# Moving instructions between rounds in an eight-stage transformer kernel on one core

## The chip, the core and the metric

The kernel runs on one core of a Trainium2 chip. The core has five engines that run their own instruction lists in order and meet through semaphores: PE (matmuls, with a separate list of weight loads, PEld), DVE (vector work), ACT (activation functions and copies), POOL (further vector work) and SP (here only transfers). Transfers are issued from the queues of SP and ACT, for weights also of POOL. PE writes its results to PSUM, from where DVE and ACT read them. The metric is the device time of one execution in microseconds (us).

## The reference

The input x is 8 batches of 256 tokens with 256 channels, float32. Four attention blocks alternate with four feed-forward blocks, each with a norm ahead and a residual behind:

```python
x = x + _L0_attn_a_ref(_layernorm(x), Wq, Wk, Wv, Wo)              # 16 heads of 16, softmax
x = x + _L0_ffn_ref(_layernorm(x), weight, scale_weight, bias)     # one linear layer
x = x + _L0_attn_b_ref(_layernorm(x), Wq, bq, Wk, bk, ...)         # 4 heads of 64, softmax
x = x + _L0_ffn_ref(...)
x = x + _L1_attn_a_ref(...)    # retention: scores * decay mask, no softmax, two rms norms behind
x = x + _L1_ffn_ref(...)       # silu(x W1) * (x W3), Hadamard transform, W2, 1024 hidden
x = x + _L1_attn_b_ref(...)    # per token: attention among 32 half-heads, softmax, difference
x = x + _L1_ffn_ref(...)
```

In the last attention each token has its own 32 x 32 score matrix (`einsum('bnqd,bnkd->bnqk', q, k)`): softmax over it, and the second half of the heads is subtracted, times a factor, from the first.

## The kernel before

The stages are named A0S (first attention), F1, B0 (second attention), F3, R1 (retention), F5, B1 (token attention) and F7. Every stage handles the 8 batches one after the other as a software pipeline written out by hand. Time is counted in slots (rounds); a batch takes 8 slots (ROUNDS). For each slot, `together` calls the `at_slot(g)` of every stage in turn on every engine, where g is the slot relative to the start of the stage. Inside, a line such as

```python
for b in due(g, -5):
    v_out(b)
```

emits step `v_out` of batch b when g = 8 b - 5. So the number says in which slot a step stands in the engine's list, and the order of the lines says in which order the steps of a slot stand. Nothing else sets an order: every engine works through its list and waits at each step for the semaphores named in `wait(name, batch, count)`. `wait("xres", b - 3, 1)` for example waits until batch b - 3 has its residual. A waiting step holds up everything behind it on its engine, transfers of that queue too. "High" and "low" are the two parts into which a float32 operand is split for PE: ACT writes the high part, DVE subtracts it to get the low part, and a product takes three matmuls.

Second attention (B0), batch b. PE: x is transposed (`x_turned`, slot -13), keys (-11), queries (-9), values (`v_out`, -5), scores (0, 2), turned row maxima (`max_turned`, 4; it waits for the values copy of batch b + 1, since both use the accumulator pb), shifted scores (6, 8), weights times values (`attend`, 9, 11), output product (14). DVE: `maximum`, `max_low`, the copy of the values with bias (`v_out`, -4), the division by the sums (`heads_out`, 10 and 12; the second product of `attend` waits for the first division), `a_low`, `residual`. F3 uses the same slots for its own batches, and POOL prepares the weights of later stages here (`prepare`, `butterfly`, `cut_mask`).

Retention (R1). One score round per slot: PE `scores_t`, DVE `masked`, PE `attend`. Between them stand the projections of later batches (`x_turned` -16, `q_out` -13, `k_out` -11, `v_out` -9) and the outputs of earlier ones. `to_tokens` and `k_out` share the accumulator pa: `k_out(b)` waits for "normed" of batch b - 3, which DVE's `heads_out` of the second half (slot 13) raises. Queries and keys go through DRAM: SP stores them (`store`, -12 and -10) and fetches them in two halves (`load_q`, `load_k`).

Token attention (B1), batch b, two score halves h. PE: `scores` (slot h), transposed probabilities (`turned`, 8), products with the values (`attend`, 9), transposed output (18), output product `y_out` (24), x transposed (-16), queries, keys, values (-14 to -12). DVE: `less_maximum` clamps the scores from PSUM (L1572), takes the maximum (L1574) and subtracts it (L1576); `weights_of` sums the exponentials (L1580), inverts, scales and multiplies (L1589). ACT: `probs` is the exponential, `turned` the copy of the channels (b_DT), `heads_out` the two copies of the heads (b_O), followed by their store, `load_k` six of the 16 key transfers per batch (SP issues ten), and the copies of q, k and v; `y_out` of an older batch waits for the copy of v (b_V), as both use pb. SP: `load_out` fetches the heads back, `load_v` the values, and the stores of q, k, v. POOL: `rstd_of`, `clipped` (waits for the load of the heads), `row_bias`, `token_heads` (with a power step, L778).

Of the kernel before, what the change touches and what calls it, by code (L numbers as in the profile page):

```python
# [36 lines left out]
TT = S // P  # L37
# [116 lines left out]
def build(nc, T, out):  # L154
    ctx = ExitStack()
    with ctx:
# [314 lines left out]
        def _(sp):  # L471
# [25 lines left out]
            for s, st in enumerate(STAGES):  # L497
                if st.kind in ("ffn0", "wide"):
                    at[s] = lambda g: None
                if st.kind == "narrow":  # L500

                    def narrow(s, st):
# [50 lines left out]
                        def at_slot(g):  # L553
                            if st.name == "attn_a0":
                                for b in due(g, 9):
                                    max_rows(b)
                                for b in due(g, -13):
                                    store(b, "kl", "kstore", "kload", KT, k_dram)
                                for b in due(g, -11):
                                    store(b, "ql", "qstore", "qload", QT, q_dram)  # L560
                                for half in range(2):
                                    for b in due(g, 4 * half - 8):
                                        load_q(b, half)
                                    for b in due(g, 4 * half - 6):
                                        load_k(b, half)
                            else:
                                for b in due(g, -12):
                                    store(b, "ql", "qstore", "qload", QT, q_dram)
                                for b in due(g, -10):
                                    store(b, "kl", "kstore", "kload", KT, k_dram)  # L570
                                for half in range(2):
                                    for b in due(g, 4 * half - 8):
                                        load_q(b, half)
                                    for b in due(g, 4 * half - 7):
                                        load_k(b, half)
# [3 lines left out]
                if st.kind == "tokens":  # L579
                    def tokens(s):  # L580
# [40 lines left out]

                        def at_slot(g):
                            for b in due(g, -7):
                                load_k(b)
                            for b in due(g, 9):
                                load_out(b)
                            for b in due(g, -7):
                                load_q(b)
                            for b in due(g, 2):
# [252 lines left out]
        def _(act):  # L882
# [13 lines left out]
            def narrow(s, st):  # L896
# [69 lines left out]
                def at_slot(g):  # L966
                    if ret:
                        for b in due(g, -8):
                            v_out(b)
# [14 lines left out]
                        for b in due(g, 26):  # L984
                            a_high(b)
                        for b in due(g, -15):
                            x_high(b)
                        for b in due(g, -13):
                            q_high(b)
                        for b in due(g, -11):  # L990
                            k_high(b)
# [85 lines left out]
            def tokens(s, st):  # L1077
# [52 lines left out]

                def at_slot(g):
                    for b in due(g, 8):
                        turned(b)
                    for h in range(TT):
                        for b in due(g, 9):
                            heads_out(b, h)
                    for b in due(g, 1):
                        probs(b, 0)
                    for b in due(g, 9):
                        store_out(b)  # L1140
                    for b in due(g, -16):
                        high(b, x_pair(s, b), pa, "xT", "vp", 1, "xh")
                    for b in due(g, 18):
                        high(b, aT, OT[1], "aT", "y", 1, "ah")
                    for b in due(g, -14):
                        out(b, "qp", "qstore", b1_qt, pb, "qev")
                    for b in due(g, -6):
                        load_k(b)
                    for b in due(g, -13):
                        out(b, "kp", "kstore", b1_kt, pa, "kev")  # L1150
                    for b in due(g, 3):
                        probs(b, 1)
                    for b in due(g, -12):
# [84 lines left out]
        def _(dve):  # L1238
# [12 lines left out]
            def narrow(s, st):  # L1251
# [127 lines left out]
                def at_slot(g):  # L1379
                    if ret:  # L1380
                        for b in due(g, 26):
                            a_low(b)
                        for b, r in running(g, 0):
                            masked(b, r)
                        for b in due(g, -15):
                            x_low(b)
                        for b in due(g, -12):
                            low(b, QT, pb, "qh", "ql")
                        for b in due(g, -10):
                            low(b, KT, pa, "kh", "kl")  # L1390
# [39 lines left out]
            def wide(s, st):  # L1430
# [70 lines left out]
                def at_slot(g):  # L1501
                    for t in range(TT):
                        for b in due(g, 1 + 2 * t):
                            maximum(b, t)
                    for b in due(g, 5):
                        max_low(b)
                    for b in due(g, -12):
                        x_low(b)
                    for c in range(CT):
                        for b in due(g, 10 + 2 * c):  # L1510
                            heads_out(b, c)
                    for b in due(g, 13):
                        a_low(b)
# [4 lines left out]
                    for b in due(g, -8):  # L1518
                        low(b, b0_Q, pb, "qh", bq, "ql")
                    for b in due(g, -4):  # L1520
                        v_out(b)
                    for b in due(g, -21):
# [15 lines left out]
            def tokens(s, st):  # L1538
# [62 lines left out]

                def at_slot(g):
                    for b in due(g, 24):
                        residual(b)
                    for b in due(g, -16):
                        low(b, x_pair(s, b), pa, "xh", "xl")
                    for b in due(g, 1):
                        less_maximum(b, 0)
                    for b in due(g, 2):
                        weights_of(b, 0)  # L1610
                        less_maximum(b, 1)
                    for b in due(g, 18):
                        low(b, aT, OT[1], "ah", "al")
                    for b in due(g, 13):
                        square_sums(b)
                    for b in due(g, 4):
                        weights_of(b, 1)
                    for b in due(g, -20):
# [168 lines left out]
        def _(pe):  # L1787

            def narrow(s, st, turn, channels_out, tokens_out, w):
# [155 lines left out]
                def at_slot(g):  # L1945
                    if ret:
# [15 lines left out]
                        for b in due(g, -13):  # L1962
                            q_out(b)
                        for b in due(g, -11):
                            k_out(b)
# [30 lines left out]
            def wide(s, turn, channels_out, tokens_out, w):  # L1996
# [102 lines left out]
                def at_slot(g):  # L2099
# [6 lines left out]
                    for c in range(CT):  # L2106
                        for b in due(g, 9 + 2 * c):
                            attend(b, c)
                    for b in due(g, -13):
                        x_turned(b)  # L2110
# [8 lines left out]
                    for b in due(g, -5):  # L2119
                        v_out(b)  # L2120
                return at_slot

            def tokens(s, st, turn, channels_out, tokens_out, w):
# [79 lines left out]

                def at_slot(g):
                    for b in due(g, 24):
                        y_out(b)
# [5 lines left out]
                    for h in range(TT):  # L2212
                        for b in due(g, 9):
                            attend(b, h)
                    for h in range(TT):
                        for b in due(g, h):
                            scores(b, h)
                    for b in due(g, 18):
# [233 lines left out]
```

## Time and profile before

| what | value |
|---|---|
| median of 3 runs | 1123.61 us (1122.81 to 1127.87) |
| the profiled execution | 1126.71 us, span 1124.9 us |
| PE busy | 915.9 us (81%) |
| PE weight loads | 776.4 us (69%) |
| DVE busy | 695.5 us (62%) |
| ACT busy | 367.3 us (33%) |
| POOL busy | 317.2 us (28%) |
| mean granted clock of PE | 0.896 |

The span reaches from the first to the last instruction of the profiled execution. Busy shares are means over stages: the second attention lies at about 250 to 464 us, retention at 464 to 603, F5 at 603 to 769, the token attention at 769 to 963 and F7 behind it, with overlaps at the seams. The granted clock is given as a share of full speed; 1.00 is 2.4 GHz and 0.50 is 1.2 GHz.

### The profile page before, as it was taken

To read this page: it belongs to the slowest core of one execution; us is meant where nothing else is said; L and a number is where in the kernel's file an instruction comes from. 1 tells how busy PE (TensorE), PEld (TensorE's weight loads), DVE (VectorE), ACT (ScalarE), POOL (GpSimd) and SP (SyncE) were. 2 spreads that over 40 slices of the span, in tenths; PEclk is the share of its full clock that TensorE was granted. 3 is DMA by queue.
4 is the path that set the end of the run, shared out by engine and by line. 5 is a ranking of instruction groups with operands and counts; after the bars stand their busy time and mean duration, and the time that the engine had idled before them with its cause. 6 is when DMAs were issued, how large, how long until landed. Compare 5 with 4: busy or idle time off the path is not lost.

```text
span 1124.9 us, 21059 instructions
## 1 busy us (share of the span) xinstructions
PE 915.9 (81%) x8018; PEld 776.4 (69%) x8018; DVE 695.5 (62%) x1291; ACT 367.3 (33%) x663; POOL 317.2 (28%) x352
## 2 busy tenths in 40 slices
PE   3589988787777678778877999997678874799998
PEld 2466665566666566656656999995566653799997
DVE  4468777646665567887775554536766767454443
ACT  2136554444222222233434332233222321332332
POOL 4202222224568474211111112100154443330000
PEclk9779998898898989898888999999777887899999
DMA  8745541001100002455440000022454445100000
GB/s 227 232 139 157 147 119 55 12 11 38 48 20 1 1 1 66 131 152 163 120 123 1 2 1 1 1 57 51 82 113 85 86 90 82 33 15 20 10 20 20
DMA packets 148580, 76.78 MB, mean 68 GB/s; under 512 B 108992, under 2 KB 139712, under 8 KB 148480
## 3 DMA queue, kind: packets, MB, share of 16 engines
q1 hardware_dynamic: 139376, 65.47, 23.1%
q0 software_dynamic: 1424, 4.98, 1.5%
q10 hardware_dynamic: 7680, 4.98, 1.5%
q8 instruction: 64, 1.05, 0.4%
q14 instruction: 36, 0.29, 0.1%
HBM read 45.77 MB, written 29.36 MB: 67 GB/s over the span
## 4 chain that ended last, share of the span: by engine, by line
PE 58%; DVE 26%; issue 7%; ACT 4%; SPq 2%; DMA 1%; POOL 1%; ACTq 0%; DVEq 0%; POOLq 0%
PE SC L380 17%; PE pb L380 8%; PE OT L380 8%; PE pa L380 4%; DVE mx L1315 3%; PE OT L2173 3%; PE OT L1890 3%; DVE OS L1488 2%; PE SC L1843 2%; PE SC L1872 2%; PE OT L2088 2%; PE SC L2161 2%; DVE pr L1576 2%; PE pa L2356 2%; DVE m L1574 2%
## 5 line engine op out<-in xcount | busy, mean ns | idle before, releaser
L380 PE MATMUL SC<-xT_h,w_h 128*128 128x256 f32 x512 | 148.3, 290 | 13.8 <-DVE xT_l L1737 11.5
L380 PE MATMUL SC<-xT_l,w_h 128*128 128x256 f32 x512 | 146.4, 286 | 0.0
L380 PE MATMUL SC<-xT_h,w_l 128*128 128x256 f32 x512 | 145.7, 285 | 0.0
L380 PEld LDWEIGHTS SC<-xT_h,w_h 128*128 128x128 f32 x512 | 98.4, 192 | 17.0 <-DVE xT_l L1737 15.1
L380 PE MATMUL OT<-w,Qs 128*128 128x256 f32 x768 | 102.9, 283 | 2.2 <-DVE Qs L1747 1.4
L1315 DVE TENSOR_REDUCE mx<-SC 128x4 f32<-128x1024 f32 x64 | 78.1, 1220 | 42.0 <-PE SC L1843 41.6
L380 PEld LDWEIGHTS SC<-xT_h,w_l 128*128 128x128 f32 x512 | 98.5, 192 | 0.0
L380 PEld LDWEIGHTS SC<-xT_l,w_h 128*128 128x128 f32 x512 | 98.2, 192 | 0.0
L380 PEld LDWEIGHTS OT<-w,Qs 128*128 128x128 f32 x768 | 95.1, 189 | 4.2 <-issue 2.6
L1743 DVE TENSOR_TENSOR hidden_f<-SC,silu_gate 128x512 f32<-128x512 f32 x64 | 44.1, 689 | 85.5 <-ACT silu_gate L1199 85.5
L1747 DVE TENSOR_TENSOR Qs<-hidden_f,Qs 128x512 fp32r<-128x512 f32 x64 | 45.2, 707 | 44.7 <-ACT Qs L1207 44.7
L1199 ACT ACTIVATE silu_gate<-SC 128x512 f32<-128x512 f32 x64 | 38.2, 597 | 101.5 <-PE SC L380 98.9
L749 POOL TENSOR_SCALAR ve<-mv 128x2 f32<-128x2 f32 x32 | 7.1, 221 | 191.3 <-DVE mv L1268 112.5
L1207 ACT ACTIVATE Qs<-hidden_f 128x512 fp32r<-128x512 f32 x64 | 40.4, 632 | 50.4 <-DVE hidden_f L1743 49.6
L2356 PE MATMUL pa<-ident,xn 128*128 128x128 f32 x192 | 34.0, 306 | 26.7 <-DVE xn L1291 20.3
L943 ACT ACTIVATE a_pr<-SC 128x1024 f32<-128x1024 f32 x32 | 32.8, 1026 | 49.2 <-PE SC L1872 49.2
L2356 PEld LDWEIGHTS pa<-ident,xn 128*128 128x128 f32 x192 | 24.4, 158 | 32.7 <-issue 21.3
L865 POOL TENSOR_SCALAR g_ve<-g_mv 128x2 f32<-128x2 f32 x16 | 3.9, 242 | 149.3 <-DVE g_mv L1722 148.8
L778 POOL TENSOR_TENSOR hr<-ssqe,half_pow 128x32 f32<-128x32 f32 x8 | 44.3, 5536 | 1.5 <-POOL ssqe L776 1.5
L943 ACT ACTIVATE pr<-SC 128x1024 f32<-128x1024 f32 x32 | 32.8, 1024 | 33.0 <-PE SC L1872 32.9
L764 POOL TENSOR_TENSOR x<-x,bo 128x512 f32<-128x512 f32 x16 | 20.4, 1273 | 67.9 <-DVE xn L1448 50.5
L1332 DVE TENSOR_TENSOR pr<-SC,mask 128x512 f32<-128x512 f32 x43 | 29.4, 685 | 16.2 <-PE SC L1872 15.9
(424 smaller groups left out, 2592.2 us busy)
## 6 DMA issues: line engine op xcount, KB each, us to landing
Qs<-q_stack SPq DMA_DIRECT2D x56, 128.0 KB, 2.8
k_stack<-KT_h SPq DMA_DIRECT2D x16, 256.0 KB, 2.4
k_stack<-KT_l SPq DMA_DIRECT2D x16, 256.0 KB, 3.1
q_stack<-QT_h SPq DMA_DIRECT2D x16, 256.0 KB, 2.2
q_stack<-QT_l SPq DMA_DIRECT2D x16, 256.0 KB, 2.8
o_groups<-b_O ACTq DMA_DIRECT2D x8, 512.0 KB, 3.0
Qs<-q_stack SPq DMA_DIRECT2D x56, 64.0 KB, 2.9
Ks<-k_stack SPq DMA_DIRECT2D x28, 128.0 KB, 3.0
```

What stands on the lines that cost most here:

```text
L380: ins = pe.matmul(out_ap, left[a], right[b], start=first and n == 0, stop=last and n == len(terms) - 1, **more)
L778: pool.tensor_tensor(hr0[:], ssqe[:], half_pow[:], ALU.pow).then_inc(sig.sem["hpow"], 1)
L943: act.activation(pr[(b * ROUNDS + r) % len(pr)][:], SC[1][:], ACT.Exp, scale=st.scale).then_inc(sig.sem["probs"], 1)
L1199: act.activation(silu_gate[:], SC[r % 2][:, 0:512], ACT.Silu).then_inc(sig.sem["g_silu"], 1)
L1207: act.activation(joined(hid[r % 2][0][:]), hidden_f[:], ACT.Copy).then_inc(sig.sem["g_hh"], 1)
L1315: dve.tensor_reduce(mx[:, t, m0:m0 + 16].rearrange("p (u g) -> p u g", u=2)[:, :, 2 * k:2 * k + 2], SC[0][:].rearrange("p (u g k) -> p u g ...
L1332: dve.tensor_tensor(to[:, :, 0, :], of[:, :, 0, :], heads, ALU.mult)
L1743: dve.tensor_tensor(hidden_f[:], SC[r % 2][:, 512:1024], silu_gate[:], ALU.mult).then_inc(sig.sem["g_hid"], 1)
L1747: dve.tensor_tensor(joined(hid[r % 2][1][:]), hidden_f[:], joined(hid[r % 2][0][:]).bitcast(F32), ALU.subtract)\
L1890: ins = pe.matmul(OT[0][32 * n:32 * n + 32, t0:S], Vr[b % len(Vr)][:, kt, 2 * r + u, :], p[:, u, kt, t0:S], start=kt == 0, stop=kt == 1, t ...
L2173: ins = pe.matmul(OT[0][:, 256 * h + 64 * n:256 * h + 64 * n + 64], b1_P[h][:, u, 8 * n:8 * n + 8, :].rearrange("p g b -> p (g b)"), own_h ...
L2356: ins = pe.transpose(ps[:, c * S + t * P:c * S + t * P + P], src[:, t, c * P:c * P + P], ident[:])
```

## The change

Only the order of steps changes: their slots and their places within a slot. No instruction is added, removed or altered.

- Second attention: PE forms the values of batches 4 to 7 one slot earlier and at another place in the slot; DVE copies them earlier in the slot, for batches 4 to 7 also one slot earlier; the second division moves from slot 12 to 13, the low part behind it from 13 to 14.
- Retention: `k_out`, its high part, its low part and its store move one slot later; on ACT the high part of x comes first in its slot; on DVE the low part of the output moves behind the mask and the low part of x.
- Token attention: both score halves stand in slot 0 and first in PE's list; DVE clamps both halves in slot 0 and forms the weights in slots 1 and 2; the low part of x goes from -16 to -15; ACT takes the exponentials in slots 0 and 1 and issues its key transfers in slot -8 instead of -6; SP issues the query load in slot -8, ahead of the key load.

```diff
 SP, retention
-                                for b in due(g, -10):
+                                for b in due(g, -9):
                                     store(b, "kl", "kstore", "kload", KT, k_dram)
 SP, token attention
+                            for b in due(g, -8):
+                                load_q(b)
                             for b in due(g, -7):
                                 load_k(b)
                             for b in due(g, 9):
                                 load_out(b)
-                            for b in due(g, -7):
-                                load_q(b)
 ACT, retention
+                        for b in due(g, -15):
+                            x_high(b)
                         for b in due(g, -8):
                             v_out(b)
...
-                        for b in due(g, -15):
-                            x_high(b)
                         for b in due(g, -13):
                             q_high(b)
-                        for b in due(g, -11):
+                        for b in due(g, -10):
                             k_high(b)
 ACT, token attention
+                    for b in due(g, 0):
+                        probs(b, 0)
+                    for b in due(g, -8):
+                        load_k(b)
                     for b in due(g, 8):
                         turned(b)
+                    for b in due(g, -16):
+                        high(b, x_pair(s, b), pa, "xT", "vp", 1, "xh")
+                    for b in due(g, 1):
+                        probs(b, 1)
                     for h in range(TT):
                         for b in due(g, 9):
                             heads_out(b, h)
-                    for b in due(g, 1):
-                        probs(b, 0)
                     for b in due(g, 9):
                         store_out(b)
-                    for b in due(g, -16):
-                        high(b, x_pair(s, b), pa, "xT", "vp", 1, "xh")
...
-                    for b in due(g, -6):
-                        load_k(b)
...
-                    for b in due(g, 3):
-                        probs(b, 1)
 DVE, retention
-                        for b in due(g, 26):
-                            a_low(b)
                         for b, r in running(g, 0):
                             masked(b, r)
                         for b in due(g, -15):
                             x_low(b)
+                        for b in due(g, 26):
+                            a_low(b)
...
-                        for b in due(g, -10):
+                        for b in due(g, -9):
                             low(b, KT, pa, "kh", "kl")
 DVE, second attention
+                    for b in due(g, -5):
+                        if b >= 4:
+                            v_out(b)
+                    for b in due(g, -4):
+                        if b < 4:
+                            v_out(b)
                     for b in due(g, 5):
                         max_low(b)
                     for b in due(g, -12):
                         x_low(b)
                     for c in range(CT):
-                        for b in due(g, 10 + 2 * c):
+                        for b in due(g, 10 + 3 * c):
                             heads_out(b, c)
-                    for b in due(g, 13):
+                    for b in due(g, 14):
                         a_low(b)
...
-                    for b in due(g, -4):
-                        v_out(b)
 DVE, token attention
+                    for h in range(TT):
+                        for b in due(g, 0):
+                            less_maximum(b, h)
                     for b in due(g, 24):
                         residual(b)
-                    for b in due(g, -16):
+                    for b in due(g, 1):
+                        weights_of(b, 0)
+                    for b in due(g, -15):
                         low(b, x_pair(s, b), pa, "xh", "xl")
-                    for b in due(g, 1):
-                        less_maximum(b, 0)
                     for b in due(g, 2):
-                        weights_of(b, 0)
-                        less_maximum(b, 1)
+                        weights_of(b, 1)
...
-                    for b in due(g, 4):
-                        weights_of(b, 1)
 PE, retention
-                        for b in due(g, -11):
+                        for b in due(g, -10):
                             k_out(b)
 PE, second attention
                         for b in due(g, 9 + 2 * c):
                             attend(b, c)
+                    for b in due(g, -6):
+                        if b >= 4:
+                            v_out(b)
                     for b in due(g, -13):
                         x_turned(b)
...
                     for b in due(g, -5):
-                        v_out(b)
+                        if b < 4:
+                            v_out(b)
 PE, token attention
+                    for h in range(TT):
+                        for b in due(g, 0):
+                            scores(b, h)
                     for b in due(g, 24):
                         y_out(b)
...
-                    for h in range(TT):
-                        for b in due(g, h):
-                            scores(b, h)
```

## Rows read from the trace of the kernel before

**Rows 1.** Busy time by stretch, the columns as in the first line; PEclk is the granted clock.
```profile
core 0: us, PE busy (x) PEld busy (x) DVE busy (x) ACT busy (x) POOL busy (x), PEclk, DMA share, GB/s
252.00:464.00 212.00, 161.47 (x1367) 137.00 (x1368) 140.33 (x263) 53.76 (x97) 120.18 (x107) 0.90 0.10 30
...
769.00:963.00 194.00, 136.89 (x1267) 105.22 (x1265) 135.95 (x174) 53.48 (x78) 63.80 (x56) 0.78 0.47 84
...
857.00:862.00 5.00, 0.02 (x1) 0.05 (x1) 4.41 (x5) 1.54 (x2) 0.43 (x1) 0.91 1.08 116
862.00:867.00 5.00, 5.00 (x24) 5.00 (x24) 4.11 (x9) 0.63 (x1) 2.38 (x5) 0.50 0.58 70
```

**Rows 2.** Chain of waits, token attention: start us, length us, engine, tile, line.
```profile
848.60 1.24 DVE pr L1572
...
852.37 1.07 ACT pr L1102
...
856.53 1.23 DVE pr L1572
...
861.25 0.59 ACT b_V L1098
...
861.98 2.90 PE pb L380 x12
864.88 6.72 PE OT L2173 x32
...
872.45 3.05 PE SC L2161 x16
```

**Rows 3.** Timeline, token attention: start us, us, engine, line, form, count, [idle before].
```profile
767.88 0.73 DVE L1556 TENSOR_SCALAR xn<-x,mv,rstd 128x256 f32<-128x256 f32 x2
...
772.89 1.23 DVE L1572 TENSOR_SCALAR pr<-SC 128x1024 f32<-128x1024 f32 x1 [1.95 <-PE SC L2161]
...
839.11 0.23 POOL L749 TENSOR_SCALAR ve<-mv 128x2 f32<-128x2 f32 x1 [2.81 <-DVE mv L1548]
...
840.28 0.74 DVE L1556 TENSOR_SCALAR xn<-x,mv,rstd 128x256 f32<-128x256 f32 x2 [0.80 <-POOL rstd L751]
...
848.35 1.92 PE L2188 MATMUL OT<-scratch,b_DT 128*32 128x128 f32 x64
...
854.10 2.19 ACTq L305 DMA_DIRECT2D b_KD<-k_tokens  x6
...
856.30 2.80 SPq L619 DMA_DIRECT2D ON<-o_groups  x4
...
860.00 5.35 SPq L611 DMA_DIRECT2D scratch<-v_tokens  x8
...
861.57 0.61 POOL L794 TENSOR_SCALAR ON<-ON 128x512 f32<-128x512 f32 x1 [12.94 <-DMA ON<-o_groups]
...
862.16 1.28 POOL L764 TENSOR_TENSOR x<-x,bo 128x512 f32<-128x512 f32 x1
...
944.47 1.23 DVE L1572 TENSOR_SCALAR pr<-SC 128x1024 f32<-128x1024 f32 x1 [3.07 <-PE SC L2161]
```

**Rows 4.** Waits of PE, second attention, then retention: us in total, times, longest.
```profile
PE pb L2050 <- DVE V L1466: 17.2, 4, 4.4
...
PEld pa L380 <- issue: 10.0, 5, 2.4
```

**Rows 5.** Chain of waits, second attention.
```profile
333.20 1.65 DVE OS L1488
```

**Rows 6.** Timelines of POOL and DVE at two meetings.
```profile
263.21 4.56 POOL L697 TENSOR_TENSOR w_l<-scratch,w_h 128x2048 fp32r<-128x2048 f32 x1
...
265.15 3.10 DVE L1677 TENSOR_SCALAR ON<-x,g_mv,g_rstd 128x256 f32<-128x256 f32 x2
...
988.91 5.46 POOL L778 TENSOR_TENSOR hr<-ssqe,half_pow 128x32 f32<-128x32 f32 x1 [0.18 <-POOL ssqe L776]
...
991.02 0.69 DVE L1747 TENSOR_TENSOR Qs<-hidden_f,Qs 128x512 fp32r<-128x512 f32 x1 [0.70 <-ACT Qs L1207]
```

**Rows 7.** DMA issues: tiles, queue, count, KB each, us to landing.
```profile
o_groups<-b_O ACTq DMA_DIRECT2D x8, 512.0 KB, 3.0
```

## Prediction

> **What bounds the kernel now.** I read the busy time and the granted clock by stage first, then the chain of waits, then each engine's timeline inside the three stages that the diff touches, then the list of waits, and last the transfers. The two large feed-forward stages are bound by PE and not touched. In the token attention no engine is full: DVE works 136 us of 194, PE 137, ACT 53, POOL 64, at a mean clock of 0.78 [rows 1], so a ring of hand-offs sets the pace. The chain shows the ring [rows 2]: clamp of score half 0 (848.60), its exponential (852.37), its weights, clamp of half 1 (856.53), its exponential, the values copy that stands behind it on ACT (861.25), the output product of an older batch (2.90), the eight probability transposes (6.72), the turn of x, the scores of the next batch (872.45). From clamp to clamp it takes (944.47 - 772.89) / 7 = 24.5 us a batch [rows 3]. PE stands still for some 5 us of each: in 857 to 862 it works 0.02 us, and in 862 to 867 it works throughout at 0.50, the lower of its two levels (1.2 GHz) [rows 1].
>
> In the second attention, between 290 and 411, PE waits four times, together 17.2 us, for the values copy on DVE before it turns the row maxima. In retention the weight loads of the key product wait five times, together 10.0 us, because the second half of the heads must first leave an accumulator that the keys share [rows 4].
>
> The sum is made on the profiled execution (1126.71 us, span 1124.9). The median of the runs shown is 1123.61, 0.3% less; I take the differences off the median. About 0.5% (5.6 us) is what a measurement of this kernel can tell from no change.
>
> **Second attention.** Nothing is added or removed. For batches from 4 on, the values product (12 matmuls; 1.45 us at the full clock, half of the 2.90 that the same form takes at the lower one [rows 2]) moves a round earlier, into a place where PE stands anyway, waiting for the division of half 0 (1.65 [rows 5]). DVE then copies the values before the low part of x and before the second division, so the turn of the maxima finds them. What is late next? First x's high and low part, 1.1 of new idle before the keys' product. Then the output product: behind the low part of the maxima DVE and ACT now have the second division and its copies, 1.65 + 0.45 + 0.6 + 0.7 with hand-offs 3.7, while PE has 2.4 left (rest of the keys' product 0.55, a turn 0.45, shifted scores 1.4): 1.3 of new idle. So of 4.3 idle and 1.45 product, 2.4 comes back: 3.3 saved. If PE then keeps the full clock, keys, turn and scores save another 2.3. Three batches have this form: 4.5 each, between the two. Batches 1 to 3 keep the product's place and gain by the order of the copies alone, 3.0 for each of the two that wait. The ends of the stage give 1.5. Sum 21.
>
> Against it stands POOL, which is busy 120 of 212 us here with weight preparation [rows 1]; a stage 20 us shorter leaves it at 63%, so it is not the bound. But one DVE normalisation took 3.10 instead of 0.73 while a POOL subtraction ran from 263.21 to 267.77 [rows 6]. After the change the feed-forward's normalisation comes some 4 us earlier in a batch, next to a POOL addition of 2.3. I charge 1 for such meetings and 2.3 in each of five batches for the bound. Taken: 20 saved, between 6 and 26.
>
> **Retention.** The keys' product goes behind the scores and products of round 6; its copy, low part and store follow one round later. The waits of 10.0 go. The product (8 matmuls, some 1.0 by the 1.45 for 12) then stands ahead of the scores of round 7; part of that is covered by DVE's normalisation in the same round, and I charge 0.6 a batch, 3.0. The copy of x ahead of the squares, with the low part of the output behind the mask, gives 0.2 a batch, 1.0. The store's lateness is hidden: keys stored in round 7 are fetched in round 1 of the next batch for the one after, and SP waits there for nothing else. Taken: 8 saved; bounds 0 (product, copy and low part all land on the mask) and 13 (the clock, which falls after the waits, stays up).
>
> **Token attention.** Both score halves now run ahead of the old output product, DVE clamps both halves in one go, and the weights find their exponential done. The ring through the output product is cut, since PE does that work while DVE is busy. What is late next is a longer ring. On ACT the six key transfers now stand between the exponential of half 0 and the channel copy of the older batch. It goes: clamp to exponential 3.77 [rows 2]; key transfers 2.19 and 0.1; channel copy and hand-off 0.7; products 1.92 and what is left of two copies 0.8 [rows 3]; store to landing 3.0 [rows 7]; four loads, from issue to POOL's clip, 5.27 (856.30 to 861.57); clip and row bias 1.87; POOL's rstd 1.17 (839.11 to 840.28); normalisation 0.65 [rows 3]. That is 21.5, with hand-offs 22.0. DVE comes to the normalisation before the next clamp, so this is the period; DVE's own 17 a batch (136 / 8) is hidden under it. PE has a ring too: two clamps 7.5, residual 0.7, weights 3.1 (853.44 to 856.53 [rows 2]), low part of x 0.7, so 12.0, then three products and the scores: 4.35 + 3.05 make 19.4 at the full clock, 8.7 + 3.05 make 23.8 at the lower. In this walk PE's longest idle is 3.2 instead of 5, so the clock should fall in some batches only: I take 22.7 for four batches. In the first period PE has nothing old to do, so its clock is low: 21.4. The last two lack row bias, rstd and normalisation (3.1) and end with the sum of squares instead (1.6): 20.5. Seven periods: 21.4 + 4 x 22.7 + 41.0 = 153.2 against 171.6, 18.4 saved. At the start the first scores no longer stand behind a turn of x, and DVE is free from 768.6 on (767.88 + 0.73 [rows 3]) instead of clamping at 772.89: 4 saved. At the end the feed-forward's x comes 21 after the last clamp instead of 19: 2 lost. Taken: 20; bounds 4 and 27. The query load ahead of the key load costs SP 0.5 in a stretch where it is idle.
>
> **Rivals.** *The shared port* (0.13). POOL's power step takes 5.46 and in the new order would lie over the first clamp's subtraction, which has two inputs in SBUF. If POOL held DVE off, that subtraction would end 2.9 later, in six periods 17: 1093. The nearest row speaks against it: the same power step runs from 988.91 to 994.37, and a DVE subtraction with two SBUF inputs inside it, at 991.02, takes its usual 0.69 [rows 6]. The Trainium skill, page "SBUF — State Buffer", section "Who interferes with whom", says that a DVE instruction with two SBUF inputs and a GpSimd instruction that reads SBUF exclude each other, and that the later one blocks fully. By that rule this rival would be the likeliest; the row at 991.02 does not agree with it for the power step.
>
> *Only the token attention pays* (0.13). If the moved division and key product become the next waits at full price, 20 remain: 1104. For it: both stages are dense. Against: each removed wait has its row.
>
> *The order is no bound* (0.06): the stalls move and the end stays, 1119 to 1126. Against: the chain passes through the links that are cut.
>
> *Slower* (0.05). A closed ring through two queues: ACT's key transfers now wait, ahead of the channel copy, for the landing of a key store; on SP that store stands behind the loads of heads and values; and the loads of heads wait for what follows the channel copy. By rows: 2.3 + 0.7 + 2.7 + 3.0 + 2.8 + 5.35 + two stores 0.8 + landing 3.0 = 20.7 [rows 3, 7], under the 22.0. It decides from 28.8 a batch on, where 7 x 4.3 lost meet the 28 of the other stages and the 2 of the ends; landings would have to be 8 us later. At 32: 1146.
>
> **How the numbers follow.** Likeliest (0.63): 1123.6 - 20 - 8 - 20 = 1076; its own range is 1058 (26 + 13 + 27 saved) to 1090. For 8 in 10 the range reaches to the partial cases: 1058 to 1106. Faster 0.63 + 0.13 + 0.13 = 0.89, same 0.06, slower 0.05.
>
> **What would show it.** Second attention: the wait before the turned maxima under 0.5, the output product waiting about 1.3. Retention: no wait before the key product, batches some 1.6 shorter. Token attention: the two clamps back to back, 22 to 24 from batch to batch, POOL waiting for the load of the heads and DVE for POOL's rstd; a first subtraction of 4 us would show the port. I am wrong if the clamps stay 24.5 apart, or if the feed-forward stages begin no earlier.

## The result and the profile after

| | before | after |
|---|---|---|
| median (lowest to highest) | 1123.21 us (1121.04 to 1127.87), 4 runs | 1090.05 us (1088.23 to 1090.53), 4 runs |
| ratio | | 0.9696, 95% interval 0.9664 to 0.9729 |
| profiled execution, span | 1126.71, 1124.9 us | 1090.53, 1088.7 us |
| granted clock of PE | 0.896 | 0.913 |

The change saves 33 us where 48 were forecast. The time lies inside the range of 1058 to 1106, at the upper end of the 1058 to 1090 that the likeliest case had for itself. Once more on another chip (after_again, below) the ratio was 0.9643 (0.9586 to 0.9700), 40 us of 1123.6. Ratios are quotients of the means of the fast runs, so the quotient of two medians differs a little from them, and slow runs (four of the eleven of the kernel before on after_again's chip) are left out.

Busy time after, the second attention and the token attention from first to last clamp, columns as in [rows 1]:

```profile
252.00:451.70 199.70, 157.59 (x1355) 131.18 (x1354) 141.67 (x262) 52.62 (x97) 120.40 (x107) 0.92 0.10 31
750.60:905.50 154.90, 117.88 (x1180) 93.03 (x1172) 114.61 (x155) 46.06 (x68) 57.27 (x49) 0.87 0.52 96
```

The same stretch of the token attention before, from first to last clamp:

```profile
772.90:944.50 171.60, 128.30 (x1172) 101.58 (x1176) 119.79 (x155) 45.21 (x67) 57.10 (x48) 0.79 0.49 88
```

PE's mean clock there is 0.87 instead of 0.79 (0.78 in the longer stretch of [rows 1]), and no engine is full here either. The lines of the changed kernel stand up to 8 further down: the clamp is L1576, the subtraction L1580. The chain of waits of one batch, clamp to clamp:

```profile
838.64 1.14 DVE pr L1576
...
842.32 0.02 ACT pr L1102
...
842.38 0.27 ACTq L305
...
844.72 0.61 ACT b_DT L1107
...
845.46 3.56 PE OT L2196 x64
...
849.04 0.61 ACT b_O L1112
...
849.67 2.63 DMA o_groups<-b_O
...
852.47 0.59 SPq L619
...
854.82 2.57 DMA ON<-o_groups
...
858.25 1.30 POOL x L764
...
860.05 0.74 POOL rstd L751
...
861.14 0.41 DVE xn L1560
861.55 1.15 DVE pr L1576
```

The chain is no longer that of [rows 2]: old output product and probability transposes are gone from it. Instead it runs through ACT's key transfers, channel copy, products, store, load, POOL's row bias and rstd, and DVE's normalisation, as the prediction walked it. DVE's timeline has the clamps at 838.56 and 861.47: 22.9 against 22.0 in the walk.

PE's waits in the second attention (285 to 450: us in total, times, longest):

```profile
PE pb L380 <- DVE aT_l L1494: 16.9, 8, 4.9
PE OT L2092 <- DVE ON L1490: 6.3, 3, 2.5
...
PE OT L2364 <- DVE ON L1681: 1.2, 2, 0.9
PE pb L2054 <- DVE V L1466: 1.0, 2, 0.9
```

The 17.2 of [rows 4] ahead of the turned maxima are 1.0 now. But the output product waits 16.9 for the low part behind the second division: 2.1 a batch in the mean, 1.1 to 3.1 in the first seven and 4.9 in the last one. In retention the 10.0 of [rows 4] ahead of the key product are 1.4 now:

```profile
PEld pa L380 <- issue: 1.4, 6, 0.4
```

The products with the masked scores wait more for the mask instead, 19.2 in 21 times after:

```profile
PE OT L1894 <- DVE pr L1333: 13.5, 14, 1.6
PE OT L1894 <- DVE r_pr L1333: 5.7, 7, 1.4
```

and 12.8 in 18 times before:

```profile
PE OT L1890 <- DVE pr L1333: 8.9, 12, 1.5
...
PE OT L1890 <- DVE r_pr L1333: 3.9, 6, 1.0
```

Stage by stage, each number the difference of two start times in the timeline of the profiled execution (us):

| run | A | E | R | S | T | F | clock |
|---|---|---|---|---|---|---|---|
| before | 171.5 | 14.2 | 139.4 | 169.6 | 171.6 | 18.9 | 0.896 |
| after | 156.7 | 19.4 | 134.5 | 164.4 | 154.9 | 21.3 | 0.913 |
| after_again | 155.0 | 19.4 | 132.3 | 165.4 | 152.7 | 21.4 | 0.918 |
| b0_alone | 155.0 | 18.4 | 138.2 | 166.8 | 166.3 | 18.9 | 0.907 |
| r1_alone | 173.3 | 16.0 | 134.5 | 167.0 | 171.9 | 18.6 | 0.890 |
| b1_alone | 171.5 | 14.2 | 148.3 | 164.3 | 155.0 | 21.4 | 0.891 |
| last_early | 154.9 | 15.8 | 127.2 | 163.0 | 153.7 | 21.4 | 0.917 |
| last_early2 | 155.0 | 16.0 | 134.5 | 164.4 | 156.3 | 21.7 | 0.906 |
| div_back | 156.7 | 16.1 | 130.1 | 163.0 | 155.2 | 21.6 | 0.915 |
| keys_behind | 158.8 | 19.3 | 132.1 | 165.4 | 145.8 | 21.3 | 0.911 |
| rstd_first | 155.0 | 19.4 | 127.1 | 163.0 | 151.5 | 21.6 | 0.922 |
| rstd_keys_ssq | 156.6 | 19.3 | 129.4 | 164.9 | 147.9 | 22.8 | 0.922 |
| last_keys | 156.8 | 16.2 | 127.6 | 165.8 | 146.5 | 21.6 | 0.923 |
| last_keys_rstd | 156.7 | 16.2 | 127.6 | 165.8 | 140.6 | 21.3 | 0.930 |

A: from the first division of the second attention to the first division of its last batch. E: from there to retention's first score; this end of one stage and start of the next is called the seam below. R: retention, to F5's first product. S: from there to the first clamp. T: first to last clamp. F: last clamp to F7's first product.

### The profile page after: what moved, and what is told of

Read it like the earlier page. It is cut to its first block, busy times and chain, and to the rows that moved or that the text cites. A ratio compares the mean times of both kernels' runs of the same rounds, so it can differ in the third digit from the quotient of the medians.

```text
span 1088.7 us, 21059 instructions
## 1 busy us (share of the span) xinstructions
PE 898.4 (83%) x8018; PEld 764.5 (70%) x8018; DVE 690.8 (63%) x1291; ACT 367.1 (34%) x663; POOL 321.0 (29%) x352
## 4 chain that ended last, share of the span: by engine, by line
PE 53%; DVE 23%; issue 8%; DMA 4%; ACT 4%; SPq 4%; POOL 3%; ACTq 1%; POOLq 0%; DVEq 0%
PE SC L380 17%; PE pb L380 8%; PE OT L380 8%; DVE mx L1315 3%; PE pa L380 3%; PE OT L1894 3%; PE SC L1847 2%; PE SC L1876 2%; DVE OS L1488 2%; PE OT L2196 2%; PE OT L2092 2%; DMA ON<-o_groups 2%; DMA o_groups<-b_O 1%; PE pa L2364 1%; ACTq L305 1%
## 5 line engine op out<-in xcount | busy, mean ns | idle before, releaser
L2196 PE MATMUL OT<-scratch,b_DT 128*32 128x128 f32 x512 | 24.9, 376 | 29.0 <-ACT b_DT L1107 29.0
L2196 PEld LDWEIGHTS OT<-scratch,b_DT 128*32 128x32 f32 x512 | 22.4, 154 | 30.4 <-issue 30.2
```

The costliest lines, as they stand in the source:

```text
L2196: ins = pe.matmul(OT[h][32 * i:32 * i + 32, P * n:P * n + P], b1_DT[:, 4 * h + n, a0:a0 + 32], b1_VB[:, 8 * i + 4 * h + n].rearrange("p e ...
```

## The experiments

A ratio is to the kernel before on the same chip, with its 95% interval. Executions of one kernel differed by 1% and more, with the granted clock: of the kernel before from 1125.22 us at 0.898 to 1136.96 at 0.881 on the first of these chips. So small differences are read from the table above, where a stage that an edit doesn't touch shows how much comes and goes by itself.

**b0_alone, r1_alone, b1_alone**: one stage's hunks of the diff each, on the kernel before.

> Only the second attention's edits on the kernel before. Read off the changed kernel, retention starts 12.2 us earlier there (463.9 to 451.7), but the third values copy of retention only 7.9 earlier: 4.2 go at the seam, where the last output product waits 4.9 for the low part behind the late second division. Theory A (the seam's loss belongs to the second attention and falls on whatever comes behind): 8 saved, 1115. Rival B (the loss belongs to retention's own edits): 12 saved, 1111. The prediction's own term was 20 saved, 1103.

> Only retention's edits on the kernel before. Theory A: its steady batches save 1.5 to 1.8 each over five periods and no seam loss comes with it: 8 saved, 1115. Rival B: the waits of the products for the mask, which grew from 12.8 to 19.2 in all, and the seam are its own: 4.9 saved, 1118. The prediction's term was 8.

> Only the token attention's edits on the kernel before. In the changed kernel the first clamp to the last takes 154.9 against 171.6, 16.7 saved; the stretch from the first product of the feed-forward ahead to the first clamp is 5.2 shorter; 2.8 is lost behind the last clamp. Theory: the ring of this stage depends on nothing ahead of it: 19 saved, 1104. Rival: part of the gain is clock that the other two edits brought (the granted clock of the whole was 0.913 against 0.896): 12 saved or less, 1111. The prediction's term was 20.

Measured: b0_alone 1114.04 against 1128.18, 0.9829 (0.9761 to 0.9896); r1_alone 1124.27, 0.9941 (0.9913 to 0.9970); b1_alone 1109.27, 0.9783 (0.9731 to 0.9835). Of 1123.6 that is 19, 7 and 24, with intervals of about 12 to 27, 3 to 10 and 19 to 30. Each part pays. The three make 50 where the whole makes 34 to 40. The widths allow for the 40, and for the 34 only at their lower ends (12, 3 and 19); whether the parts take from each other is not settled. The stage times are sharper. b0_alone has A and E much as the whole has them (A 16.5 shorter, E 4.2 longer of the whole's 5.2), so most of the loss at the end comes with the second attention's own edits, as theory A had it; the 12.3 that are saved there come out at rival B's size all the same. b1_alone has T at 155.0 as the whole has, with the other two edits absent: the rival that its gain is borrowed clock falls. Its R, 148.3 in a stage that it doesn't touch, is 9 longer than before's: so much comes and goes. r1_alone (R 4.9 shorter, 7 by the ratio) doesn't tell A from B; its E is 1.8 longer without any edit of the second attention.

**last_early**: only the last batch's second division goes back.

```diff
                     for c in range(CT):
                         for b in due(g, 10 + 3 * c):
-                            heads_out(b, c)
+                            if c == 0 or b < B - 1:
+                                heads_out(b, c)
+                    for b in due(g, 12):
+                        if b == B - 1:
+                            heads_out(b, 1)
```

(`a_low` likewise: slot 13 for the last batch.)

> The changed kernel, but for the last batch alone the second division of the second attention goes back to slot 12 and the low part to 13, ahead of retention's low part of the queries on DVE. Theory: there the division stood 4.0 behind that low part (it began at 441.05, its product was done at 437.43), the output product waited 4.91, and PE's clock fell to 0.50 from 458 to 470 after it. The wait falls to about 2, retention starts some 3 earlier, and with the clock up to 3 more come back: 1084 to 1087. Rival: retention is held by its masks and its query fetch, nothing is gained: 1090.

> The changed kernel with only the last batch's second division early, again, beside the three others on one chip. Theory: 0.954 of the kernel before, as in its first measurement, with retention at 127 from first score to F5's first product. Rival: that was the chip, and 0.964 to 0.970 comes out as for the changed kernel.

Measured: 1081.22, 0.9541 (0.9496 to 0.9587); on another chip 1088.20, 0.9642 (0.9599 to 0.9684). The changed kernel:

```profile
440.12 0.75 DVE L1306 SCALAR_TENSOR_TENSOR QT_l<-pb,qscale,QT_h 128x512 fp32r<-128x512 f32 x1 [4.00 <-ACT QT_h L919]
...
441.05 1.76 DVE L1488 RECIPROCAL OS<-OT 128x256 f32<-128x256 f32 x1
```

DVE stands 4.00 at retention's low part of the queries, and the division behind it in the list starts late. With it ahead, the wait of the output product falls from 4.9 to 0.9 and E from 19.4 to 15.8 and 16.0 in the two runs: 3.4 to 3.6 saved, shown. The first ratio promised more, and it did not come again. My theory that the clock falls behind this wait is refuted by the busy time of PE from retention's first score to its third values copy: the changed kernel in its two executions (after, after_again),

```profile
451.70:473.60 21.90, 19.21 (x153) 14.75 (x152) 15.47 (x39) 4.54 (x9) 4.03 (x7) 0.69 0.44 129
```

```profile
450.50:468.50 18.00, 15.12 (x153) 11.71 (x152) 15.43 (x39) 4.55 (x10) 4.03 (x7) 0.91 0.53 158
```

and the kernel without the wait in its two (last_early, last_early2):

```profile
448.02:466.05 18.03, 15.14 (x153) 11.69 (x152) 15.39 (x39) 4.54 (x9) 4.04 (x7) 0.91 0.56 156
```

```profile
450.70:472.60 21.90, 19.21 (x153) 14.75 (x152) 15.48 (x39) 4.55 (x10) 4.03 (x7) 0.69 0.45 130
```

The same 153 matmuls take 21.9 at 0.69 or 18.0 at 0.91, with the long wait ahead of them and without it.

**after_again**: the changed kernel beside the next three.

> The changed kernel once more, on the chip of the following three, so that they have it beside them. Theory: its ratio to the kernel before comes out near 0.970 again, retention (first score to F5's first product) takes 134 with PE's clock near 0.5 ahead of the third values copy, and the clamps stand 22.1 apart on average. Rival: the small gain of its first measurement was that chip's, and 0.955 to 0.962 comes out here, as the sum of the three parts alone would have it.

Measured: 1085.96, 0.9643 (0.9586 to 0.9700). The interval excludes neither the theory's 0.970, at its upper end, nor most of the rival's 0.955 to 0.962. R is 132.3 and the clock behind the seam 0.91, so the theory's detail is wrong; the stages hold within 2.2 each (A 155.0, E 19.4, T 152.7). The 1.7 of A lie in its first period alone, 24.51 at a clock of 0.93 in the first execution and 22.88 at 1.00 here.

**div_back**: the second division in slot 12 and the low part in 13 for all batches; the values still first.

```diff
-                        for b in due(g, 10 + 3 * c):
+                        for b in due(g, 10 + 2 * c):
                             heads_out(b, c)
-                    for b in due(g, 14):
+                    for b in due(g, 13):
                         a_low(b)
```

> The changed kernel, but the second division of the second attention is back in slot 12 and the low part in slot 13, for all batches; the values still move first. Theory (the values copy ahead is what removes the wait before the turned maxima, the later division is a second, separate edit): that wait stays gone (under 1 each), the output product's waits for the low part (2.1 a batch, 4.9 for the last) fall to about 1, the low part of the maxima comes 2.2 later and the shifted scores wait for it; the middle comes out even, and the end gains what the last batch alone gains: 1075 to 1082. Rival: without the later division the turn of the maxima waits again, some 3 a batch: 1090 to 1100.

Measured: 1082.43, 0.9587 (0.9537 to 0.9636). PE's waits in the second attention:

```profile
PE OT L2364 <- DVE ON L1681: 9.4, 6, 3.2
...
PE pb L2054 <- DVE QT_l L1306: 2.1, 1, 2.1
PE SC L2071 <- DVE MT_l L1479: 1.7, 3, 0.8
PE pb L380 <- DVE aT_l L1494: 1.6, 2, 0.9
PE pb L2054 <- DVE V L1466: 1.0, 2, 0.9
```

The wait for the values stays at 1.0 without the later division: the copy's place alone removes it. The output product's wait falls from 16.9 to 1.6, but the turn of F3's x now waits 9.4 (1.2 in the changed kernel), not the shifted scores as I expected (1.7). A is 156.7 either way. So the later division earns nothing in the middle that can be told from what A does by itself (154.9 to 158.8 in the ten executions with it); it moves a wait from one product to another, and at the end it costs 3.3 (E 16.1).

**keys_behind, rstd_first, rstd_keys_ssq**: links of the new ring.

```diff
 keys_behind, ACT
-                    for b in due(g, -8):
-                        load_k(b)
...
                     for b in due(g, 9):
                         store_out(b)
+                    for b in due(g, -7):
+                        load_k(b)
 rstd_first, POOL
-                    for b in due(g, -19):
+                    for b in due(g, -21):
                         rstd_of(b)
 rstd_keys_ssq: both, and on DVE square_sums from slot 13 to 16, behind less_maximum(b, 0)
```

> The changed kernel, but ACT issues its six key transfers behind the two head copies and their store (slot -7) instead of between the first exponential and the channel copy. Theory (the ring of the prediction sets the period): the channel copy comes 2.2 earlier, and with it products, store, loads, clip, rstd and the next clamp: 22.1 becomes 20 a batch, some 12 saved in six periods; the keys land at about 5 before the scores need them. Rival: the products at the lower clock set the period, or the scores now wait for the keys: 0 to 4 saved, or a loss.

> The changed kernel, but POOL's rstd of the token attention stands ahead of the clip of the heads (slot -21), so it no longer waits for the load. Its input is ready some 3 before that load lands. Theory: from the clip to the clamp the path goes over the squares on ACT (0.63) and their sum on DVE (0.69) instead of row bias, rstd (0.24 + 0.73) and normalisation, 1.1 shorter: 7 saved in six periods, clamps 21 apart. Rival: the load of the heads is not what the clamp waits for, nothing is saved.

> The changed kernel with both edits, and the sum of squares on DVE between the two clamps of the next batch: then no step ahead of the first clamp waits for the load of the heads, and the ring through the loads is cut. Theory: what is left is PE's own ring, estimated at 19.4 at full clock and 23.8 at the lower, and DVE's 17: clamps 19.5 to 20.5 apart, some 12 to 17 saved, and PE waits for its scores no more. Rival: the power step on POOL then begins later, the turn of the older batch waits for it, and the period stays at 22: nothing saved.

Measured beside after_again (1085.96, 0.9643, T 152.7): keys_behind 1079.37, 0.9571 (0.9510 to 0.9632), T 145.8; rstd_first 1082.62, 0.9616 (0.9555 to 0.9677), T 151.5; rstd_keys_ssq 1089.07, 0.9655 (0.9601 to 0.9710), T 147.9. The key transfers are a link: T is 6.9 shorter, and 146.5 again in last_keys below. (The intervals of the two ratios overlap, so this rests on T.) That is little more than half of the 12 I expected, since I overlooked that ACT's exponential runs beside their issue and is left when they go. In the changed kernel:

```profile
842.32 1.06 ACT L1102 ACTIVATE pr<-pr 128x1024 f32<-128x1024 f32 x1 [6.26 <-DVE pr L1580]
842.38 2.23 ACTq L305 DMA_DIRECT2D b_KD<-k_tokens  x6
```

An estimate from these rows: 2.2 less 1.1 in six or seven periods is 7 to 8. rstd alone gives 1.2 in T, where after_again and after differ by 2.2: not told from nothing. In the third kernel the rival came in, in part: T is 2.0 longer than with the keys alone, though 4.8 shorter than in after_again. The power step starts only behind the sum,

```profile
831.77 5.46 POOL L778 TENSOR_TENSOR hr<-ssqe,half_pow 128x32 f32<-128x32 f32 x1 [0.18 <-POOL ssqe L776]
...
839.28 1.06 POOL L786 TENSOR_TENSOR ON<-ON,hr 128x512 f32<-128x512 f32 x1 [0.27 <-POOL hr L782]
```

and PE's turn of the heads waits for it:

```profile
840.40 0.90 PE L2365 MATMUL OT<-ident,ON 128*128 128x128 f32 x3 [4.13 <-POOL ON L786]
```

And the end of the kernel is later: from F7's first product to the last instruction it takes 167.9 for 161.6 in after_again. The last batch's sum of squares stands behind F7's first steps on DVE now, at 921.09, 7.4 after F7's first product; in after_again it stands 2.8 ahead of it (919.60). PE then waits for POOL's heads within F7, as it doesn't in after_again:

```profile
PE OT L2365 <- POOL ON L786: 4.7, 1, 4.7
```

**last_keys, last_keys_rstd**: last_early with keys_behind, and with rstd_first too.

> last_early and keys_behind together. Theory: the gains lie in different stages and add: 7 less than last_early, ratio 0.948. Rival: the clamp ring then stands on PE at the lower clock, nothing added.

> Both and POOL's rstd ahead of the clip; the sum of squares stays where it was, so the power step is not late. Theory: from clip to clamp 1.1 less, the clamps 19.5 to 20 apart instead of 20.5: 3 to 6 less than last_keys, ratio 0.944. Rival: with the load earlier PE's own work (19.4 at full clock) is the bound and the scores are waited for: nothing added.

Measured: last_keys 1074.60, 0.9526 (0.9484 to 0.9568), last_keys_rstd 1069.13, 0.9503 (0.9452 to 0.9554), T 146.5 and 140.6. The first lies 13.6 us in medians under last_early2, more than the 7 expected; in the profiled pair T gives 9.8, and 6.9 lie in R, which the edit doesn't touch. With the keys off the path, rstd comes with 5.9 in T, 0.8 in each of seven periods, where alone it gave 1.2 in all of them. The medians differ by 5.5, but the two intervals overlap, so that rstd pays here is likely and not shown. In medians the last is 19 us under last_early2 on the same chip, and its interval lies below both of the changed kernel's: the fastest version here, 5% under the kernel before.

## Why the prediction was right, and where it was too high

**Token attention** (20 forecast). Right in mechanism and size: S 5.2 shorter (4), T 16.7 (18.4), F 2.4 longer (2): 19.5. Part of the size may be luck, since S was 2.8 and T 5.3 shorter in b0_alone too, which doesn't touch them; but T is 152.7 to 156.3 in the six executions with this edit and without a further one in its ring, and 166.3 to 171.9 in the three without it. The periods are 19.8, 21.4, 22.7, 24.0, 22.9, 21.5, 22.6. PE's clock was put somewhat too high: the products and copies of the walked batch take 4.2 (845.46 to 849.64) instead of 2.7, because PE stands 5.5 for the channel copy ahead of them, not 3.2, and runs them at 0.54. POOL waits for the load of the heads (64.9 us in five waits) and DVE for POOL's rstd (5.9 in five), as said. keys_behind confirms the ring by taking a link out of it. The walk's ring of PE takes the scores at 3.05 at both clocks, from a row that ran at 0.62; no reading here hangs on it.

**The shared port** did not come in: the subtraction, with two inputs in SBUF, takes its usual 1.23 inside the power step. POOL's row, then DVE's:

```profile
838.34 5.61 POOL L778 TENSOR_TENSOR hr<-ssqe,half_pow 128x32 f32<-128x32 f32 x1 [0.18 <-POOL ssqe L776]
```

```profile
841.06 1.23 DVE L1580 TENSOR_TENSOR pr<-pr,m 128x1024 f32<-128x1024 f32 x1
```

**Second attention** (20 forecast). Here the prediction failed, in two terms. "The ends of the stage give 1.5": E is 5.2 longer. The division was followed through a batch in the middle, but not through the last one, where retention's low part of the queries stands in its place; last_early gives 3.4 to 3.6 of it back, and the 1.6 to 1.8 that stay (16.0 for 14.2) are seen in r1_alone as well, with retention's edits alone. And the middle gives 14.8 (16.5 in after_again) for the 19.5 less 1 charged. The first five periods are 3.2, 3.4, 5.3, 3.1 and 0.9 shorter (first division at 278.10 and 305.84 before, 275.69 and 300.20 after, and so on), against 3.0 twice and 4.5 three times: the first four make 15.1 of 15. The sixth and seventh are 0.7 and 0.4 longer. The fifth, where 4.5 were taken, holds the output product's longest wait of the middle, 3.07. There DVE's low part meets POOL's weight preparation; first DVE's row, then POOL's:

```profile
377.48 2.58 DVE L1494 TENSOR_TENSOR aT_l<-ON,aT_h 128x512 fp32r<-128x512 f32 x1 [0.69 <-ACT aT_h L1054]
```

```profile
375.87 5.39 POOL L694 TENSOR_SCALAR scratch<-scratch 128x2048 f32<-128x2048 f32 x1
```

The same subtraction takes 0.69 at 443.96. This one meeting costs 1.9 where 1 was charged for all. It is not the whole of the fifth period. In the changed kernel, then in div_back, where the output product doesn't wait there, the period is:

```profile
367.27:392.55 25.28, 20.23 (x170) 17.23 (x168) 16.75 (x28) 5.50 (x10) 19.85 (x11) 0.86 0.01 2
```

```profile
366.21:387.07 20.86, 17.80 (x170) 14.74 (x168) 15.54 (x28) 5.72 (x10) 15.97 (x8) 1.00 0.01 2
```

Of the 4.4 between them 2.4 is PE's own time for the same 170 matmuls, at 0.86 and 1.00. So the full clock, which the 4.5 counted in part, did not stay in this period. div_back gives these 4.4 back in the next two periods (20.78 and 23.59 for 18.77 and 21.03), at 0.84 and 0.78, with a wait of 3.2 ahead of F3's turn. Whether the meeting brings the lower clock was not tried. The output product's new wait was put at 1.3 and is 2.1; in div_back it goes and the wait of F3's turn comes for it, and A is the same, so the middle loses nothing by it that can be told. With 2.4 gained ahead of the first division, which the other runs don't settle, the stage gives 9.6 to 12. The bounds given with the 20 don't follow from its terms either: 2.3 less in each of five batches would make 8.5 for the 6, and three batches at 5.6, with the 6 and 1.5, no more than 24.3 for the 26.

**Retention** (8 forecast). R is 4.9 shorter in the profiled pair; the eleven executions with this edit range from 127.1 to 134.5, the three without from 138.2 to 148.3. The waits of 10.0 fell to 1.4, and 6.4 came back ahead of the mask, more than the 3.0 charged. In medians 7 (3 to 10): right as far as it can be read.

**The clock.** That PE keeps the full clock when its waits shorten was counted in as 2.3 a batch at most. It goes up on the mean (0.896 to 0.913), but the same kernel gets it or not at the same place, worth 4 us at the seam alone. How much of the 33 against 40 of the two measurements is that stays open. The 0.5% that the prediction takes for the resolution of one measurement is too small: the two ratios of last_early differ by 1%.

## What to carry to other kernels

Follow a moved step through the first and the last batch too: there other stages' steps stand in its slot, and an in-order engine waits for them. The last division and the last sum of squares both lost time that way. A step that only moves a wait from one product to another (the later division) is told from one that removes it by undoing it alone. When a stage is a ring of hand-offs, write the ring down link by link, and ask of each link what runs beside it: a transfer issue of 2.2 over an exponential of 1.06 was worth 1.1 a period here. A second link may show its worth only after the first is gone: rstd's 1.2 became 5.9, by one profile each.

## What the runs showed of the hardware

The granted clock at one place of one kernel was 0.69 in one execution and 0.91 in another, with the same 153 matmuls, and both values were seen with a wait of 4.9 ahead and with one of 0.9: a single pair of profiles can't price a clock effect of 4 us.

What DVE loses to POOL depends on POOL's instruction. A DVE subtraction took 2.58 instead of 0.69 under a TENSOR_SCALAR of POOL (375.87), and 1.23, its usual time, under the power step. The Trainium skill, page "SBUF — State Buffer", section "Who interferes with whom", says that a DVE instruction with two SBUF inputs contends with a GpSimd instruction that reads SBUF. The row at 377.48 agrees in that it is slowed, but it ends at 380.06, ahead of POOL's end at 381.26, so it is not held off for the whole of it; the power step in this kernel slows nothing.
